# A graph network kernel: the one-hots of the last nine slots wait for the end of the window before, instead of for the first matmul of their own window

## What is computed

```python
src = concatenate([src, loops]); dst = concatenate([dst, loops])
deg = segment_sum(ones_like(dst), dst, n)
dinv = where(deg > 0, rsqrt(deg), 0)
norm_edge = dinv[src] * dinv[dst]
h = x
for W, b in ((W1, b1), (W2, b2), (W3, b3)):      # 256 -> 512 -> 512 -> 256
    msg = (h @ W)[src] * norm_edge[:, None]
    h = relu(segment_sum(msg, dst, n) + b)
return layernorm(x + h)
```

## Time and profile before

| | |
|---|---|
| time, median of 3 runs | 2474.43 us (2469.54 to 2475.84) |
| span of the profiled execution | 2970.2 us |
| PE busy in it | 2388.2 us, 80% |
| POOL busy | 1696.7 us, 57% |
| DVE busy | 994.1 us, 33% |
| ACT busy | 718.8 us, 24% |
| PE waiting for `take_sum` in phase 0, window to window | 37.5 us (L1640) and 34.1 us (L1636) |
| mean granted TensorE clock, of full speed | 0.902 |

### The profile page before, as it was taken

One profiled execution on the slowest core, in us unless ns is written; L12 is line 12 of the kernel. 1 busy time (PEld: TensorE's weight loads), 2 busy tenths in 40 slices (PEclk: granted clock), 3 DMA queues, 4 the chain that ended last, 5 costly groups with the idle time before them and its releaser, 6 DMA issues.

```text
span 2970.2 us, 39333 instructions
## 1 busy us (share of the span) xinstructions
PE 2388.2 (80%) x12137; PEld 1629.3 (55%) x12138; DVE 994.1 (33%) x1126; ACT 718.8 (24%) x1501; POOL 1696.7 (57%) x1768
## 2 busy tenths in 40 slices
PE   7866687778687788779788888788888789988897
PEld 6754465555555666334333334333343378888887
DVE  8775222122122221234233323333331223323232
ACT  7411122222121221112121222212221123333332
POOL 4366555555455554666666666666666655555553
PEclk9787899889898999989899989889999989999999
DMA  5445554444454554667767666766767666666663
GB/s 180 137 131 170 160 163 143 145 147 142 126 161 144 153 153 141 197 211 226 221 210 225 208 217 212 224 213 211 225 211 255 186 186 187 191 184 184 181 189 97
DMA packets 219981, 537.93 MB, mean 181 GB/s; under 512 B 38444, under 2 KB 88483, under 8 KB 219827
## 3 DMA queue, kind: packets, MB, share of 16 engines
q0 software_dynamic: 117216, 365.08, 42.2%
q1 hardware_dynamic: 83955, 123.53, 12.0%
q10 hardware_dynamic: 18656, 47.20, 5.0%
HBM read 448.05 MB, written 87.61 MB: 180 GB/s over the span
## 4 chain that ended last, share of the span: by engine, by line
PE 51%; another core or an unknown queue 20%; issue 15%; DVE 6%; ACT 4%; ACTq 1%; DVEq 1%; POOL 1%; DMA 1%; SPq 0%; POOLq 0%
PE ps_acc L1640 9%; PE ps_d L1640 9%; PE ps_o L1689 6%; PE ps_acc L1636 5%; PE ps_d L1739 4%; PE ps_T L1727 3%; PE ps_T L1728 3%; PE ps_h L1727 2%; PE ps_h L1728 2%; PE ps_h L1680 2%; PE ps_l L1710 2%; PE ps_d L1594 1%; ACT big L1404 1%; PE ps_e L1710 1%
## 5 line engine op out<-in xcount | busy, mean ns | idle before, releaser
L727 POOL DMA_INDIRECT rows<-table,idx x1249 | 1200.6, 961 | 768.5 <-issue 369.9
L949 DVE SCALAR_TENSOR_TENSOR sel<-ps_e,firsts,dstT 128x1152 f32<-128x1152 f32 (+1 forms) x214 | 303.2, 1417 | 1200.9 <-PE ps_acc L1640 313.9
L1640 PE MATMUL ps_acc<-rows,sel 128*128 128x512 f32 (+2 forms) x1496 | 632.7, 543 | 76.7 <-DVE acc L1029 37.5
L727 POOL DMA_INDIRECT rows<-table_parts,idx x483 | 456.4, 945 | 395.4 <-PE ps_acc L1636 168.0
L1640 PE MATMUL ps_d<-rows,sel 128*128 128x512 f32 (+2 forms) x1190 | 526.6, 557 | 19.4 <-issue 12.0
L1640 PEld LDWEIGHTS ps_acc<-rows,sel 128*128 128x128 f32 x1496 | 281.2, 210 | 218.3 <-issue 183.5
L1689 PE MATMUL ps_o<-low,hT 128*128 128x512 f32 (+1 forms) x784 | 293.0, 519 | 66.7 <-ACT hT L1347 49.1
L1636 PE MATMUL ps_acc<-rows,sel 128*128 128x256 bf16 (+1 forms) x1533 | 257.2, 287 | 55.8 <-DVE acc L1029 34.1
L1640 PEld LDWEIGHTS ps_d<-rows,sel 128*128 128x128 f32 x1190 | 209.7, 198 | 149.5 <-issue 133.3
L1689 PEld LDWEIGHTS ps_o<-low,hT 128*128 128x128 f32 x784 | 154.6, 202 | 187.8 <-issue 118.7
L1739 PE MATMUL ps_d<-big 128*128 128x256 bf16 x1470 | 241.6, 284 | 8.4 <-issue 8.4
(11 more groups left out here) (190 smaller groups left out, 2340.5 us busy)
## 6 DMA issues: line engine op xcount, KB each, us to landing
built<-big SPq DMA_DIRECT2D x84, 384.0 KB
low<-built ACTq DMA_DIRECT2D x84, 384.0 KB
rows<-table,idx POOLq DMA_INDIRECT x1249
table<-made SPq DMA_DIRECT2D x49, 256.0 KB
acc<-table SPq DMA_DIRECT2D x49, 256.0 KB
built<-big SPq DMA_DIRECT2D x28, 416.0 KB
low<-built ACTq DMA_DIRECT2D x28, 416.0 KB
table_parts<-big SPq DMA_DIRECT2D x24, 384.0 KB
```

The lines of the kernel that those rows point to most:

```text
L727: pool.indirect_dma_start(out=to, out_offset=None, in_=its[0:nodes, :], in_offset=bass.IndirectOffsetOnAxis(ap=idx[:, of, k:k + 1], axis=0 ...
L949: v.scalar_tensor_tensor(to[:, k:k + FRONT, :], numbers.unsqueeze(1).broadcast_to([P, FRONT, P]), firsts[:, bass.ds(t, 1)], dstT[:, bass.d ...
L1640: return mm(to[:, 0:w], sel[:, k, :], rows_of[phase][:, k, 0:w] if first is None else first, start=start, stop=stop)
```

## The change

One wait changes. It stands ahead of the one-hots of slots 9 to 17, on DVE, in `prepare`:

```diff
@@ def prepare(n, t, base, part, to=sel):
                     if part == 0:
                         v_.wait_ge(slots_used, n * USED - 1)
                     else:
-                        v_.wait_ge(opened, n + 1)
+                        v_.wait_ge(window_done, n)
                 k = part * FRONT
```

## The result

| | median | lowest to highest |
|---|---|---|
| before | 2474.14 us | 2469.54 to 2475.84, 4 runs |
| after | 2457.01 us | 2452.3 to 2461.51, 4 runs |

By the medians the change takes away 17.1 us; the prediction said 15. The ratio on record is 0.9917, with an interval of 0.9896 to 0.9938. It is not the quotient of the two medians, which is 0.9931; of 2474 us it is 20.5 us, with an interval of 15.3 to 25.7. A second comparison, further down, gives a ratio of 0.9929, 17.6 us, and 19.2 us by its medians. So the gain is known to a few microseconds only: 17 to 21.

A forecast was written before the change was run, and what follows sets the result against it. PE was taken to bound phase 2, DVE the first windows of phase 0. Terms 11.3 + 4.9 = 16.2 us, 13.5 if scaled to the timed median; 15 was taken, giving 2459 us, range 2450 to 2473.

The forecast's parts named there:

- Who waited for it: nothing: At L949, the nine one-hots of 1.42 us: no engine waits for them; a wait costs through what stands behind on DVE.
- Phase 2, 11.3 us: Thirteen holes of PE shrink as the chain from DVE starts earlier: 6.7 us ahead of piece 12, 4.6 ahead of piece 1.
- the two behind the loop's jump: Two phase 2 group starts behind a jump back in PE's loop: pauses over 4 us, holes of 1.03 and 0.67 go whole.
- First windows of phase 0, 4.9 us: Removing DVE's pause saves 1.6 us for each of three sums, after the back one-hots of windows 2, 3 and 5.
- The bound from above: First windows of phase 0: POOL's idle time before windows 3 to 6 limits the saving to 7.3 us.
- the gathers pace the first windows: Rival for the start of phase 0: only phase 2 counts, 9.4 to 11.3 us, giving 2463 to 2465; chance 0.18.
- the scaling by 2474 / 2970: Whole sum: 16.2 us from the stretched profile, scaled to the timed median, would be 13.5; 15 was taken, between the two.
- Rest of phase 0, and phase 1, nothing: After the back one-hots DVE waits again or only reads loop registers, so removing the pause there counts 0.
- Earlier one-hots and gathers, nothing: One-hots starting 0.9 to 1.6 us sooner run beside other gathers without slowing them; term 0.
- The rival of a held gather: Phase 1, 48 windows: earlier one-hots hold a gather, 1.2 us each, all 48 +58 us, up to 2517; chance 0.04.
- The count blocks are next: Rival in phase 2: ACT then waits for the blocks' transfer, the 6.7 us fall away, 2466; chance 0.10.

The follow-up runs named there:

- e5_before: The kernel before, unchanged, run and profiled again on an undisturbed chip; 2478.81 us, ratio 1.0001 to before.

## Why the prediction was right

The time was right: 2457.01 us, where 2459 was predicted and 2450 to 2473 was the range; the gain is 17 to 21 us instead of 15. That it came so close is in part luck, as the steps show:

**"Who waited for it: nothing".** Right for what the change touches, and shown: with the old wait and the layer norm first, the gain is there all the same. On an undisturbed chip the view names one wait for L949, 4.9 us (`e5_before` and after alike). It stands ahead of the very first window (PE at 121.40 in `e5_before`), before any of the changed waits.

**Phase 2, 11.3 us.** The mechanism was right and the places too: thirteen holes, at pieces 12 and 1. What the holes gave back was 10.5 us, from 15.1 to 4.6. Ahead of piece 12 it was 5.7, predicted 6.7; ahead of piece 1 it was 4.8, predicted 4.6. The 6.7 are a misreading. Several holes were measured to the start of a L1728, as the rows show (2942.19 and 2885.35 in the earlier trace rows), but PE resumes 0.2 us earlier, with a L1727:

```profile
2941.97 0.38 PE L1727 MATMUL ps_h<-pairs_r,rows_r 128*128 128x256 f32 x1 [0.72 <-ACT rows_r L1422]
```

Read so, the seven holes of the prediction's own trace are 0.72 to 0.90 us and add up to 5.7, as on the undisturbed chip; the two behind the loop's jump are 0.81 and 0.45, not 1.03 and 0.67, and the term would have been 9.8. In `e5_before` these two are 1.40 and 0.39 and went whole; the other four became 0.7 to 0.8 us shorter. And the term had a part missing: phase 2 alone gained 13.4 us by the ratio, 14.9 by the medians and 18 in the traces, of which 4 to 7 are matmuls that take less time. The prediction put the clock at nothing without a reason. Rows that spoke of it were to be had before: a hole of 1.92 us and a mean clock of 0.96 in the phase.

**First windows of phase 0, 4.9 us.** This step failed. The pauses went as predicted and the lead was even larger, 6.3 us at the sixth sum. But it is a lead towards a point that the gathers set, and most of it was given back within three windows; 2.7 us or nothing remains. The bound from above, POOL's idle time of 7.3 us in the earlier trace rows, did not exist on an undisturbed chip. The rival "the gathers pace the first windows" was right about this term, though not about the sum. The prediction gave it 0.18 and had quoted what spoke for it, POOL issuing without a pause in windows 1 and 2. It trusted the rows against it, from an execution with a span 20% too long.

So two errors cancelled, and that is the luck: 4.9 us in phase 0, of which 2.7 or none arrived, and 2 to 4 us too few in phase 2, with the scaling by 2474 / 2970 between them, which was right for neither. Take 11.3 alone and it would have been 2463.

**Rest of phase 0, and phase 1, nothing.** Right: 1.0001 for phase 1 alone.

**Earlier one-hots and gathers, nothing.** Right. In the changed kernel a gather beside the earlier back one-hots (177.28 to 178.69, shown above) takes 0.95 us, as the one behind it does:

```profile
177.56 0.95 POOL L727 DMA_INDIRECT rows<-table,idx  x1 [0.31 <-issue]
178.81 0.95 POOL L727 DMA_INDIRECT rows<-table,idx  x1 [0.30 <-issue]
```

In the trace of after, 34 gathers lie wholly inside the time of back one-hots, and all of them took 0.94 to 0.95 us. The rival of a held gather, which would have cost up to 58 us, is refuted by phase 1 alone at 1.0001. The Trainium skill (SBUF — State Buffer, "Who interferes with whom") says that a DVE instruction with at most one input in SBUF, outside the 2-port modes, does not contend with GpSimd. L949 compares numbers from PSUM with indices from SBUF, and the trace agrees.

**The count blocks are next.** Refuted: at all 13 places ACT went from the start of the square root to that of the widening in 0.20 to 0.27 us in the trace of after (1999.24 to 1999.44 in the one shown), and at the place shown with the layer norm first in 0.20 us too (1996.77 to 1996.97). The blocks were there.

What stays open is whether the 2.7 us of phase 0 are real; the interval reaches from 5.7 us to none. That moving the layer norm beats the change is also not settled by the times: 0.9900 with both against 0.9917 and 0.9929 for the change, with intervals that overlap. In the traces its phase 2 is 5 to 8 us shorter, and all thirteen holes are gone. And why the traces give 18 us for phase 2 where the timed runs give 13 to 15 is open.

## What to carry to other kernels

If no one waits for the result of an instruction that itself waits, look at what stands behind it in the same queue, and follow that across engines to the one that bounds the stage. If that chain is short of time, put it ahead of the work that is needed later; it is worth as much as a better wait.

An engine's idle time counts as room only if it is there in an undisturbed execution. Where the profiled span is far above the timed median, ask of every gap that the sum needs whether the disturbance made it, and let counts and durations decide: about 16 gathers for each of 109 windows (1249 and 483 in the trace of after), at 0.96 + 0.30 us, are 20 us a window. From the 3rd sum to the 9th it was 19.8 us a window in `e5_before` and 20.0 in after, whatever DVE did.

A hole of PE in a stage that PE bounds can have a second price, the matmuls behind it that run at the lower clock. Here 10.5 us less of idle time came with 4.0 us less of busy time in the first pair of traces and 11 us with 7 on average, and 47 us more with 22 more.

## What the hardware showed that I had not expected

The same kernel took 2479 us on one chip and 3015 on another, with "remote" waits of up to 5.9 (POOL), 17.3 (DVE) and 25.6 us (ACT). What causes them no run here shows.

Whether a hole of PE brings the lower clock is not settled by its length alone. Of the 12 holes of 1.83 to 1.93 us in the three traces with the old wait, 8 were followed by 3.4 us at 1.2 GHz and 4 by none, in the same place of the same loop (rows above). Holes of up to 1.40 us never were.
